# Last four token groups' steps brought closer together, and the softmax denominators placed ahead of the root's spread, in the slot stage of a decoder layer

## What is computed

```python
x = layernorm(x + mamba(x, ...))              # selective scan
x = layernorm(x + slots(x, ctx, ...))         # slot attention, 3 rounds
x = layernorm(x + experts(x, ...))            # 8 experts, the best one

# slots: k_proj, v_proj from rmsnorm(ctx), 77 context rows per sequence
for _ in range(3):
    sn = rmsnorm(slots, slot_norm_w)
    scores = einsum('bkd,bmd->bkm', sn @ Wq.T, k_proj) * SCALE
    attn = softmax(scores, axis=-2)                # over the 128 slots
    attn = attn / (sum(attn, axis=-1) + EPS)       # over the 77 rows
    slots = gru_cell(einsum('bkm,bmd->bkd', attn, v_proj), slots, ...)

# experts
route = sigmoid(x @ Wr + br);  best = argmax(route);  gate = max(route)
out = gate * (gelu(x @ W1[best]) @ W2[best])
```

## Time and profile before

| | us |
|---|---|
| median of 3 runs | 1630.61 (1629.01 to 1631.13) |
| profiled execution | 1634.47 |
| its span, first to last instruction | 1632.6 |
| busy in the span: PE, DVE, POOL, ACT | 1443.6, 1272.2, 1252.6, 1096.3 |
| PE's idle time ahead of the first expert matmul (1459.96) | 27.62 |

### The profile page before, as it was taken

The page is one execution under the profiler, slowest core; times in us unless marked ns, Lnnn a source line. Parts: engine busy times, 40 slices in busy tenths (PEclk is TensorE's granted clock), DMA queues, the critical chain, the costliest instruction groups (busy, mean ns, idle before and its releaser), DMA issues. The chain is left out here.

```text
span 1632.6 us, 22044 instructions
## 1 busy us (share of the span) xinstructions
PE 1443.6 (88%) x6146; PEld 876.3 (54%) x6146; DVE 1272.2 (78%) x2207; ACT 1096.3 (67%) x2118; POOL 1252.6 (77%) x861
## 2 busy tenths in 40 slices
PE   4889999999999989998998699999999999529994
PEld 1333343434343434343333377778777787429993
DVE  1999999999999999999999257777777777714552
ACT  4778877887788778887786366666666666204552
POOL 1899999999999999999999334477777766434665
PEclk8999999999999999999999799999999999759997
DMA  5455455545554555455543353303418000036771
GB/s 170 147 182 177 164 183 184 176 158 180 181 178 161 178 183 180 160 187 188 175 151 124 90 190 129 138 30 135 152 42 327 14 8 12 11 111 193 210 206 38
DMA packets 126058, 236.92 MB, mean 145 GB/s; under 512 B 13490, under 2 KB 76917, under 8 KB 125952
## 3 DMA queue, kind: packets, MB, share of 16 engines
q1 hardware_dynamic: 121408, 227.21, 42.4%
q0 software_dynamic: 4544, 8.47, 1.5%
HBM read 180.89 MB, written 55.66 MB: 145 GB/s over the span
## 5 line engine op out<-in xcount | busy, mean ns | idle before, releaser
L388 POOL TENSOR_TENSOR hc<-state,c_rows 128x1024 f32<-128x1024 f32 x256 | 598.7, 2359 | 49.9 <-DVE state L585 40.3
L585 DVE TENSOR_TENSOR_SCAN state<-ps_da,inp 128x512 f32<-128x512 f32 x512 | 593.2, 1205 | 29.5 <-ACT ps_da L481 29.5
L704 PE MATMUL ps_y<-hc,ident 128*128 128x512 f32 x1024 | 495.1, 623 | 55.4 <-POOL hc L388 55.3
L481 ACT ACTIVATE ps_da<-dt,a_neg 128x512 f32<-128x512 f32 x512 | 345.1, 688 | 81.6 <-DVE state L585 79.1
L704 PEld LDWEIGHTS ps_y<-hc,ident 128*128 128x128 f32 x1024 | 195.6, 198 | 298.7 <-issue 214.9
L574 DVE TENSOR_TENSOR inp<-dtx,ps_b 128x1024 f32<-128x1024 f32 x192 | 230.7, 1202 | 39.2 <-POOL dtx L359 22.9
L1063 POOL TENSOR_TENSOR rs<-ms,m_half 128x4 f32<-128x4 f32 x48 | 59.2, 1232 | 136.2 <-DVE ms L1250 136.0
L371 POOL TENSOR_TENSOR inp<-dtx,b_rows 128x1024 f32<-128x1024 f32 x64 | 150.8, 2356 | 0.1
L627 PE MATMUL ps_misc<-x1T,w_conv 128*128 128x512 f32 (+3 forms) x256 | 118.4, 607 | 21.5 <-ACT x1T L414 21.5
L1180 ACT ACTIVATE ex<-sc,nmx,ctx_r 77x128 f32<-77x128 f32 x192 | 92.4, 482 | 64.9 <-DVE nmx L1263 64.9
L487 ACT COPY ps_b<-b_rows 128x512 f32<-128x512 f32 x192 | 111.1, 579 | 36.6 <-DVE inp L574 35.1
(11 more groups left out here) (234 smaller groups left out, 2731.5 us busy)
## 6 DMA issues: line engine op xcount, KB each, us to landing
b_rows<-bc_rows SPq DMA_DIRECT2D x128, 512.0 KB, 4.6
c_rows<-bc_rows SPq DMA_DIRECT2D x128, 512.0 KB, 3.9
sorted_x<-pad_rows SPq DMA_DIRECT2D x8, 4160.0 KB, 16.0
w<-in_L_ffn_W SPq DMA_DIRECT2D x78, 256.0 KB
vw<-vw_rows SPq DMA_DIRECT2D x16, 462.0 KB
vw_rows<-vw_out SPq DMA_DIRECT2D x16, 384.0 KB
xrow<-sorted_x SPq DMA_DIRECT2D x39, 130.0 KB, 2.3
x_tok<-in_x SPq DMA_DIRECT2D x16, 256.0 KB, 3.8
```

What stands on the lines that cost most here:

```text
L388: pool.tensor_tensor(hc[:, n % RING], state[:, n % RING], over_c(c_rows[:, slot, n % 2]), ALU.mult).then_inc(hc_ready, 1)
L481: act.activation(ps_da[u % DA_RING][:], dt[:, par, c], ACT.Exp, scale=a_neg[:, c, n:n + 1]).then_inc(da_ready, 1)
L585: dve.tensor_tensor_scan(state[:, n % RING, c], ps_da[u % DA_RING][:], inp[:, n % RING, c], 0.0, ALU.mult, ALU.add).then_inc(state_ready, 1)
L704: ins = pe.matmul(ps_y[:, c], ident[:], hc[:, n % RING, c], start=False, stop=n == NS - 1)
```

## The change

There are three parts.

1. **Order in every beat.** PE does den(n-1) ahead of root_spread(n); DVE does rdn(n-1) ahead of sc, mx and nmx of unit n, and pre(n-2) ahead of rse and rser.
2. **The last four groups.** A second function `end(n, late)` gives groups 12 to 15, and their steps take three beats: 0 residual and make_u (make_u at the end of PE's beat); 1 read_u, statistics, root, scaling, norm and tanh; 2 highest, chosen expert, count, ranks, places, labels and scatter. `LAST` falls from N+9 to N+6. The tiles have four sets of buffers, and the waits that guarded two sets go. The scatter of group 11 comes one beat sooner, behind its labels.
3. **Stores.** Group 14's scatter moves into the slot stage, behind its last labels; only group 15's stays at the start of the expert stage.

The core of the diff:

```diff
-    LAST = N + 9
+    LAST = N + 6
-    tok = [sb(f"tok{k}", [P, GB, P + NE]) for k in range(2)]
+    tok = [sb(f"tok{k}", [P, GB, P + NE]) for k in range(FOUR)]
...
+    def end(n, late):
+        g = ready.get(n - late)
+        return g if g is not None and g >= END else None
...
 # POOL
             g = post(n, 5)
-            if g is not None and g < END:
+            if g is not None:
                 labels(g)
+                if g == END - 1:
+                    scatter(g)
+            g = end(n, 1)
+            if g is not None:
+                end_root(g)
+            g = end(n, 2)
+            if g is not None:
+                labels(g) if g < NG - 2 else last_labels(g)
+                if g < NG - 1:
+                    scatter(g)
...
 # ACT, behind copy_scores(n)
+            g = end(n, 1)
+            if g is not None:
+                read_u(g, 0)
+                read_u(g, 1)
...
 # DVE, ahead of kept(n - 3)
+            g = end(n, 2)
+            if g is not None:
+                highest(g)
+                chosen_expert(g)
+            g = end(n, 1)
+            if g is not None:
+                statistics(g)
+                end_veps(g)
...
+            if live(n - 1):
+                denominators(n - 1)
             if live(n):
                 maxima(n)
-            if live(n - 1):
-                denominators(n - 1)
...
 # PE
+            if live(n - 1):
+                den(n - 1)
             if live(n):
                 root_spread(n)
-            if live(n - 1):
-                den(n - 1)
...
+            g = end(n, 2)
+            if g is not None:
+                count(g)
+            g = end(n, 0)
+            if g is not None:
+                make_u(g, n)
             if live(n + 1):
                 ssq(n + 1)
...
 # expert stage, POOL
-        for lane in range(2):
-            pool.wait_ge(last_dest[lane], 1)
+        pool.wait_ge(last_dest[1], 1)
```

More of the change, by code:

```diff
@@ L827, in slot_stage @@
     ids = sb("ids", [P, 2, GB])
-    tok = [sb(f"tok{k}", [P, GB, P + NE]) for k in range(2)]
[L829 to L839, removed]
+    tok = [sb(f"tok{k}", [P, GB, P + NE]) for k in range(FOUR)]
+    lg = [sb(f"lg{k}", [P, GB, NE]) for k in range(FOUR)]
+    route = [sb(f"route{k}", [P, GB, NE]) for k in range(FOUR)]
+    top = [sb(f"top{k}", [P, GB]) for k in range(FOUR)]
+    cand = [sb(f"cand{k}", [P, GB, NE]) for k in range(FOUR)]
+    which = [sb(f"which{k}", [P, GB]) for k in range(FOUR)]
+    hot = [sb(f"hot{k}", [P, NE, GB]) for k in range(FOUR)]
+    upto = [sb(f"upto{k}", [P, NE, GB]) for k in range(FOUR)]
+    place = [sb(f"place{k}", [P, NE, GB]) for k in range(FOUR)]
+    stats2 = [sb(f"stats2_{k}", [P, GB, 6]) for k in range(FOUR)]
+    mv2 = [sb(f"mv2_{k}", [P, GB, 2]) for k in range(FOUR)]
+    rstd2 = [sb(f"rstd2_{k}", [P, GB]) for k in range(FOUR)]
     ps_s = psum("ps_s", [P, T])
@@ L924, in post @@
     def post(n, late):
-        return ready.get(n - late)
+        g = ready.get(n - late)
+        return g if g is not None and g < END else None
+    def end(n, late):
+        g = ready.get(n - late)
+        return g if g is not None and g >= END else None
     def h_in(n):
@@ L1104, in labels @@
             hold(pool, choice_made, ev(CHOICE, "top", g), passed2[1])
[L1105 removed]
+            pool.tensor_scalar(row[k][:, :, P], top[g % FOUR][:], 0.5, 0.5, ALU.mult, ALU.add).then_inc(labels_made, 1)
             pool.tensor_copy(row[k][:, :, P + 1], ids[:, k]).then_inc(labels_made, 1)
@@ L1147, in _ @@
             if g is not None:
-                logits(g) if g < END else end_root(g)
+                logits(g)
             g = post(n, 5)
-            if g is not None and g < END:
+            if g is not None:
                 labels(g)
+                if g == END - 1:
[8 more added lines that the diff above has]
+                    scatter(g)
             for g in ctx_roots(n):
@@ L1213, in route_tanh @@
                 act.wait_ge(end_logits, ev(END_LOGITS, "logits", g - END))
-            need(act, choice_made, ev(CHOICE, "less", g - 2))
-            act.activation(route[g % 2][:], lg[g % 2][:], ACT.Tanh, scale=0.5).then_inc(routed, 1)
+            act.activation(route[g % FOUR][:], lg[g % FOUR][:], ACT.Tanh, scale=0.5).then_inc(routed, 1)
         square(0)
@@ L1412, in _ @@
             g = post(n, 2)
-            if g is not None and n < N:
+            if g is not None:
                 statistics(g)
-                if g >= END:
-                    end_veps(g)
+            g = end(n, 2)
+            if g is not None:
+                highest(g)
+                chosen_expert(g)
+            g = end(n, 1)
+            if g is not None:
+                statistics(g)
+                end_veps(g)
             if live(n - 3):
@@ L1439, in _ @@
                 chosen_expert(g)
-            g = post(n, 3)
-            if g is not None and g >= END:
+            g = end(n, 1)
+            if g is not None:
                 end_scaled(g)
                 end_norm(g)
-            g = post(n, 2)
-            if g is not None and n >= N:
-                statistics(g)
-                end_veps(g)
+            g = end(n, 2)
+            if g is not None:
+                ranks(g)
+                destinations(g)
+            if live(n - 2):
+                new_in(n - 2)
             if live(n):
                 normaliser(n)
-            if live(n - 2):
-                new_in(n - 2)
     @blk.tensor
```

73 lines of the change are left out of this document (33 added, 40 removed).

## The result

The changed kernel takes 1660.4 us (median; 1659.35 to 1662.39) against 1630.84 in the same comparison: a ratio of 1.0185, interval [1.0167, 1.0203], 30 us slower. The forecast was no change.

| stretch | before | after | difference | forecast |
|---|---|---|---|---|
| start to the root `rs` of beat 47 | 1378.70 | 1401.96 | +23.3 | -2.4 |
| to the cast of group 11 | 25.5 | 29.0 | +3.5 | +4.0 |
| to the first instruction of the expert stage | 37.9 | 42.4 | +4.5 | +2.7 |
| expert stage | 190.5 | 186.1 | -4.4 | -4.0 |

The account below looks back on a forecast made before the run. PE's own list bounds the beats at clock 1.00, so only its waits can be won; then POOL's stores. Terms +4.0 - 6.4 + 6.7 - 4.0 = +0.3 on 1630.61 gave 1630.9 us, 8-in-10 range 1624 to 1637.5.

Parts of the forecast that it names:

- Part 1, the mechanism: In beats, rdn ahead of sc ends den_spread's wait; without make_u, the loop through at makes ssq wait.
- the 0.53 that it gave: Gain claimed per make_u beat from DVE's idle time, 0.28 + 0.34 - 0.09; twelve such beats gain 6.4 us.
- The loop's term: Beats without make_u: loop through at of 9.31 against 9.19, 0.12 lost in each of 33, +4.0 us.
- the bound of 0.25: Upper bound of the loss per beat without make_u, if at's release costs 0.17; +8.3 us over these beats.
- the loop costs more: Rival: handovers root_spread to sc and at to ssq cost more, say 0.30 lost a beat, 1636.8 us; chance 0.20.
- Part 2: Last four groups: group 11's cast 4.0 later, then POOL and DVE alternating; POOL ends 6.7 us later.
- Its lower bound: Low end for the last four groups, stated as +5.8 us, from group 11's cast varying by 0.7 either way.
- The turns: Behind group 11's cast, POOL's store and root alternate with DVE's scaling, norm, ranks and places: 9.74 us a round, three rounds.
- the drain: From POOL's end to the first instruction of the expert stage: 4.92 us, claimed to stay.
- Part 3: Stores: one store leaves the start of the expert stage, so xrow is issued sooner; -4.0 us, between -2.8 and -5.8.
- as the bound had it: Expert stage: SP is busy with weights until 1451.97, so xrow's earlier issue gains at most 5.8 us.
- the ring order: Expert stage: SP's DMAs share a ring per DMA engine, consumed in order, so xrow stands behind all weights; term then -2.8.

Follow-up runs that it names:

- the kernel with the filled wait: The changed kernel with one unused matmul of 384 columns on PE ahead of ssq in beats without make_u: 1637.66 us, ratio 1.0039 to the kernel before.

## Why the prediction was wrong, step by step

**Part 1, the mechanism, was right in direction.** rdn ahead of sc took the wait at den_spread away, at became the loop, and ssq waits for it, as the text said. Of the twelve make_u beats, which took 10.2 to 10.5 before, three win the 0.53 that it gave as they stand (9.71 or 9.72), six would without the fall (11.39 less 1.67), and three take 9.99 to 10.13.

**The loop's term was mis-sized:** 9.46, not 9.31. The steps, from DVE's rows of the changed kernel with PE's above:

```profile
1252.17 0.68 DVE L1276 TENSOR_TENSOR sc<-sc,ps_rs 77x512 f32<-77x512 f32 x1 [0.39 <-PE ps_rs L1533]
...
1253.80 0.69 DVE L1308 SCALAR_TENSOR_TENSOR rh<-tr,hnb 128x512 f32<-128x512 f32 x1
1254.40 1.11 DVE L1302 SCALAR_TENSOR_TENSOR at<-ex,rser,ps_d 77x128 f32<-77x128 f32 x4
```

den to root_spread is 0.81 as given, root_spread to sc 0.75 (0.71 given), sc to rh 1.63 as given, rh to at 0.60 (0.66 given), at 1.11. At ends at 1255.51, and ssq starts at 1255.66: 0.15 for a release to which I gave 0.04, from the one row of a DVE instruction behind ACT. And from that ssq on to the next den it is 4.41, not 4.34 (1246.20 to 1250.61). So the loss is 0.28 in a plain beat, beyond the bound of 0.25. Worth 33 x 0.16 = 5.3 us, this alone would have given 1636.2, slower and still inside the range of 1624 to 1637.5; it is the rival "the loop costs more", close to its price of 0.30.

**The step that failed is one that wasn't there.** The sum took every duration at the clock of its row, and moved a wait from one place in PE's list to another at the price of its length. The kernel before has a granted clock of 1.00 with waits of 0.20 to 0.44 in every beat, but these rows tell only of a wait ahead of den_spread. Moved ahead of ssq, waits of 0.51 to 0.69 let the clock fall thirteen times, 21.7 us that no term, bound or rival held. Without them the time would have been some 1638.7 (1660.4 - 21.7), just above the range's upper end of 1637.5; the kernel with the filled wait took 1637.7.

**Part 2** gave +6.7, and the trace of the changed kernel +8.0. (Its lower bound should read 6.7 - 0.7 = +6.0, not +5.8; nothing hangs on it.) Group 11's cast came 3.5 later (4.0 given). The turns were as described, 10.2 in the mean rather than 9.74, and the drain 5.25, not 4.92. The order of DVE in one turn, from the root on POOL to the places:

```profile
1438.04 0.19 DVE L1361 TENSOR_TENSOR lg<-tok,rstd 128x32 f32<-128x32 f32 x1 [7.21 <-POOL rstd L1098]
...
1439.52 0.18 DVE L1400 TENSOR_TENSOR place<-ps_r,base 128x32 f32<-128x32 f32 x1
...
1440.49 0.21 DVE L1410 TENSOR_REDUCE dest_f<-place 128x4 f32<-128x32 f32 x1
```

**Part 3** gave -4.0, and the expert stage is 4.4 shorter. xrow is issued 11.3 behind the stage's first instruction in place of 15.7, not "some 10". SP is busy with the weights until 1483.01 + 0.38, 10.0 behind the stage's first instruction, as the bound had it; xrow stands 1.3 behind that. Of this SP's waits put 0.5 down to the landing of the stores, where it was 5.0 before, so the landing hardly holds SP any more.

```profile
1483.01 0.38 SPq L1719 DMA_DIRECT2D w<-in_L_ffn_W  x1
1484.65 3.81 SPq L1714 DMA_DIRECT2D xrow<-sorted_x  x4
```

The rows then came through: the first expert matmul starts 14.2 behind the stage's first instruction, 17.8 before, which is 3.7 of the 4.4 (timeline of PE):

```profile
1487.54 1.30 PE L1879 MATMUL ps_t<-ident,xrow 128*128 128x128 f32 x4 [22.61 <-DMA xrow<-sorted_x]
```

(By the ring order that the Trainium skill states, "DMA: Bandwidth & Descriptors", section "Queues, rings and completion order", this term was worked out as -2.8; the measured one is larger, and no row shows in which order the transfers went.)

## What to carry to other kernels

A wait on TensorE costs more than its length where the clock falls behind it. Here that depended on its place: 0.69 us idle between matmuls of 128 columns and more cost nothing but itself in any beat, and 0.52 beside matmuls of one column cost 1.67 more in 13 of 45 beats. So when an edit moves a wait on a busy PE, look at what stands on both sides of its new place, and look at the granted clock in windows of some us, not over the span (0.942 before, 0.928 after). When a loop closes through a shared bank, another bank for the smaller user is worth a try before the order is turned: with it, and the stores split, the order that cost 23 us won 26.

## What was not expected of the hardware

- Two groups of 128-column matmuls behind a wait still run at full speed when the clock falls later: at 1240.97 and 1241.47 den_spread and z take 0.66 and 1.06, and only xn at 1242.37 takes 1.87.
- In the plain beats ahead of the first make_u the fall comes in every second beat, with the same 0.52 of idle time ahead of ssq in each. Why not in each stays open, as does why the kernel with scores ahead of ssq took from 1638.68 to 1660.60 in its four runs.
- A matmul that computes nothing, put into a wait, made the changed kernel 22.7 us faster.
